# Graph attention and expert block on one core: the second graph's lag in the opening stage goes from two steps to six

## The reference

```python
def gat_layer(x, adj, W, a_self, a_neigh, b):          # twice per batch, 8 heads of 32
    feat = jnp.einsum('nf,hfo->hno', x, W)
    e = attn_self[:, :, None] + attn_neigh[:, None, :]
    e = leaky_relu(e, 0.2) + -1e10 * (1.0 - adj)[None, :, :]
    out = jnp.einsum('hnm,hmo->hno', softmax(e), feat) + b[:, None, :]
    return elu(concat_heads(out))
x = x + graph(ctx_512, layernorm(x))     # adj is the normalised x itself
x = x + block(layernorm(x))              # rmsnorm, q/k/v, rotary, causal attention, out, top-2 of 8 experts
```

## Time and profile before

| | |
|---|---|
| median of 3 runs | 664.06 us (659.31 to 664.84) |
| the profiled execution | 662.46 us, of which the span is 660.7 us |
| opening stage, by the trace | 0 to about 127.6 us of the span |
| TensorE busy over the span | 606.6 us (92%) |
| VectorE busy over the span | 434.6 us (66%) |
| GpSimd busy over the span | 305.9 us (46%) |
| ScalarE busy over the span | 268.6 us (41%) |
| products for the clock (L637) | 131, all between 12.8 and 118 us |

### The profile page before, as it was taken

One profiled execution on the slowest core, in us unless ns is written; L12 is line 12 of the kernel. 1 busy time (PEld: TensorE's weight loads), 2 busy tenths in 40 slices (PEclk: granted clock), 3 DMA queues, 4 the chain that ended last, 5 costly groups with the idle time before them and its releaser, 6 DMA issues.

```text
span 660.7 us, 10362 instructions
## 1 busy us (share of the span) xinstructions
PE 606.6 (92%) x3271; PEld 437.0 (66%) x3271; DVE 434.6 (66%) x1279; ACT 268.6 (41%) x653; POOL 305.9 (46%) x588
## 2 busy tenths in 40 slices
PE   3799899489799999989799999989999998999998
PEld 2278468236586789736597789746768873666886
DVE  4997499389756387689757387655653656664463
ACT  2462563065566333055556333036750204675020
POOL 1493594278853240268854150267730027863000
PEclk9999899799999999998989999999999999999999
DMA  8920000000000000000000000000000000000000
GB/s 276 387 73 2 1 1 4 12 4 2 1 1 0 1 2 1 24 9 1 0 2 1 0 1 1 3 15 1 1 1 0 1 9 8 1 0 1 1 0 17
DMA packets 8729, 14.41 MB, mean 22 GB/s; under 512 B 908, under 2 KB 7372, under 8 KB 8420
## 3 DMA queue, kind: packets, MB, share of 16 engines
q1 hardware_dynamic: 8676, 13.76, 5.9%
HBM read 12.70 MB, written 1.05 MB: 21 GB/s over the span
## 4 chain that ended last, share of the span: by engine, by line
PE 64%; DVE 20%; issue 6%; POOL 4%; ACT 4%; DMA 1%; DVEq 0%; POOLq 0%; SPq 0%; ACTq 0%
PE bank L615 14%; PE bank L513 10%; PE bank L573 6%; PE bank L559 5%; PE bank L592 4%; PE ob L487 4%; PE tb L476 3%; PE bank L637 2%; DVE tt L958 2%; PE bank L588 2%; PE bank L584 2%; DVE ssq L1023 2%; ACT prob L726 2%; DVE m L1020 2%; DVE qT L958 1%
## 5 line engine op out<-in xcount | busy, mean ns | idle before, releaser
L559 PE MATMUL bank<-wqkv_sb,hT 128*128 128x512 f32 x192 | 95.0, 635 | 0.4 <-ACT v_sb L702 0.4
L726 ACT ACTIVATE prob<-bank,sneg,rms 128x128 f32<-128x128 f32 (+1 forms) x128 | 63.9, 508 | 59.6 <-DVE sneg L1052 59.4
L836 POOL TENSOR_TENSOR m<-early,rope_s 128x256 f32<-128x256 f32 x80 | 73.5, 942 | 30.8 <-ACT early L707 30.6
L513 PE MATMUL bank<-m,wgu_sb 128*128 128x128 f32 (+1 forms) x480 | 85.6, 329 | 0.8 <-DVE early L1099 0.8
L794 POOL TENSOR_SCALAR tt<-tt,gmn 128x256 f32<-128x256 f32 x96 | 67.3, 710 | 37.4 <-DVE gmn L958 37.0
L852 POOL TENSOR_SCALAR prob<-prob,srcp 128x128 f32<-128x128 f32 (+1 forms) x128 | 53.1, 432 | 51.4 <-DVE srcp L1123 51.2
L513 PEld LDWEIGHTS bank<-m,wgu_sb 128*128 128x128 f32 x480 | 71.0, 191 | 9.0 <-DVE early L1099 2.2
L573 PE MATMUL bank<-kT,qT 128*128 128x128 f32 (+1 forms) x256 | 61.5, 356 | 1.8 <-ACT prob L726 1.8
L559 PEld LDWEIGHTS bank<-wqkv_sb,hT 128*128 128x128 f32 x192 | 35.9, 199 | 36.9 <-issue 34.0
L615 PE MATMUL bank<-wo_sb,qT 128*128 128x256 f32 x256 | 59.0, 382 | 0.7 <-ACT qT L732 0.7
L707 ACT ACTIVATE early<-bank 128x512 f32<-128x512 f32 x40 | 24.1, 602 | 84.4 <-PE bank L559 84.4
(11 more groups left out here) (200 smaller groups left out, 1217.0 us busy)
## 6 DMA issues: line engine op xcount, KB each, us to landing
wqkv_sb<-wqkv_dram SPq DMA_DIRECT2D x1, 3072.0 KB, 12.0
wgu_sb<-wgu_dram SPq DMA_DIRECT2D x2, 1408.0 KB, 11.5
wo_sb<-wo_dram SPq DMA_DIRECT2D x1, 2048.0 KB, 18.2
wd_sb<-wd_dram SPq DMA_DIRECT2D x1, 1408.0 KB, 15.6
out_dram<-rows SPq DMA_DIRECT2D x8, 128.0 KB, 1.7
xin<-x_dram SPq DMA_DIRECT2D x3, 256.0 KB, 2.7
rows<-gat_rows_dram SPq DMA_DIRECT2D x2, 256.0 KB, 2.8
kT<-x_dram SPq DMA_DIRECT2D x1, 256.0 KB, 4.5
```

The source lines that it names most:

```text
L513: mm = pe.matmul(ps[:, m * N + c0:m * N + c1], wgu_sb[:, m, k, n * P:(n + 1) * P], tokT[:, k, c0:c1], start=(k == 0), stop=(k == KT - 1))
L559: mm = pe.matmul(ps[:, :], hT[:, k, t * P:(t + 1) * P], wqkv_sb[:, k, c * G * HD:(c + 1) * G * HD], start=(k == 0), stop=(k == KT - 1))
L726: ins = act.activation(prob[:, n % 5, i * nk:(i + 1) * nk], ps[:, i * nk:(i + 1) * nk], ACT.Exp, bias=sneg[:, n, i:i + 1], scale=rq(g, t, ...
L836: ins = pool.tensor_tensor(dst[:, :, c, :], src[:, :, 1 - c, :], s_, ALU.mult)
```

## The change

Only constants of the schedule change. Batch 1's graph runs six steps behind batch 0's in the opening stage. The setup of the second layer's term columns is one step earlier (14 and 15). The rotary tables, the mask and the expert rows are made at steps 25, 26 and 27. The unread products are 94 and not 131, with other counts for each step: none at step 43, ten at step 30 and ten at step 47, fourteen at step 8 as before, one where there were two.

```diff
-BEHIND = 2
-TERMS1_AT, ROPE_AT = (15, 16), (39, 40, 41)
-WAKE = {2: 3, 7: 4, 8: 14, 19: 3, 20: 3, 21: 3, 22: 3, 23: 3, 24: 3, 25: 3, 26: 3, 27: 3, 28: 3, 30: 4, 31: 14, 43: 20}
-WAKE.update({s: 2 for s in tuple(range(9, 19)) + tuple(range(32, 43))})
+BEHIND = 6
+TERMS1_AT, ROPE_AT = (14, 15), (25, 26, 27)
+WAKE = {2: 3, 4: 2, 6: 3, 7: 3, 8: 14, 25: 3, 26: 3, 27: 3, 28: 4, 29: 4, 30: 10, 47: 10}
+WAKE.update({s: 1 for s in tuple(range(9, 25)) + tuple(range(31, 47))})
```

## The result

| | before | changed |
|---|---|---|
| median | 664.45 us (4 runs) | 691.44 us (4 runs, 687.41 to 695.46) |
| profiled execution | 662.46 us, span 660.7 | 689.64 us, span 687.8 |
| granted clock over the span | 0.977 | 0.916 |
| `hT` begun (L1007) | 126.6 us | 156.0 us |
| first q/k/v product (L559) | 128.5 us | 160.5 us |

The ratio is 1.0419 (95% interval 1.0346 to 1.0491): the change makes the kernel 4% slower. The forecast was 655 us. The opening stage is 32.0 us longer, and the tails give 4.9 back.

A forecast was written before the change was run, and what follows sets the result against it. VectorE was taken to set the opening stage's pace, GpSimd and TensorE close behind. 7.0 us from the schedule and 1.8 from the clock, 8.8 off 662.46, gave 653.7; 655 was predicted for the median, range 648 to 662.

The forecast's parts named there:

- The start: Opening of layer 0: batch 0's first leaky relu at 16.5 us against 20.51, 4 us earlier.
- The fourteen products at step 8: Unread products before batch 0's fifth unit: 3.0 us at the high clock, 3.5 allowed, VectorE idle some 2.5.
- Steps 9 to 41: Middle of both layers: VectorE sets the pace; batch 0's layer 0 ends at 59.7 us, step 35 at 92.4.
- TensorE's list for these steps: Steps 13 to 18: TensorE's 13.8 us and GpSimd's 12.2 do not bound VectorE's 18.3.
- the last rival: One-graph steps: the clock falls, steps take 3.1 to 4.0 us, 17 us lost, 671; chance 0.09 with other losses.
- I charge nothing for the dropped products.: Whole opening stage: 37 dropped unread products, 8.0 us of TensorE time, counted as covered by VectorE or the turn.
- The turn: Layer 0 to layer 1, steps 19 to 27: batch 1 drains under it, first leaky relu at 74.0 us against 74.58.
- the 7 us promised: End of the opening stage: `hT` ends at 120.5 us against 127.46, 7.0 us earlier from the schedule.
- Rival 1: One-graph steps: GpSimd's 2.03 us a unit sets the pace, 4.4 less gain, 659; 0.31 together with late pair operands or drain.
- The setup's place: Rotary setup, mask and expert rows in the turn: 5.1 us of VectorE, 2.3 us too long for its cover.
- The tails' start: First q/k/v product: 1.98 us at the high clock instead of 3.78, 1.8 us gained from the clock.
- The forecast's own sign of being wrong: Steps 28 to 41: VectorE waiting for unit products or granted clock under 0.9; or the wait before L1001 still near 3.9 us.

The follow-up runs named there:

- lag6_filled_k8: lag6_filled with six instead of fourteen unread products at step 8; median 656.29 us, 0.9886 of the kernel before.
- lag6_filled: lag6_three with twelve instead of three unread products at steps 13 and 27; median 662.04 us, 0.9943 of the kernel before.
- lag2_termsonly: The kernel before with only the term columns made one step earlier (14 and 15); median 670.74 us, ratio 1.0104.
- lag6_three: The changed kernel with three unread products instead of one in steps 9 to 24 and 31 to 46; median 673.89 us, 1.0156 of the kernel before.
- lag2_ropemid: The kernel before with term columns at 14 and 15 and rotary tables, mask and expert rows at 25 to 27; median 670.43 us, ratio 1.0094.
- lag2_ropeonly: The kernel before with only rotary tables, mask and expert rows moved to steps 25 to 27; median 660.94 us, ratio 0.9965.
- lag4_three: lag6_three with a lag of four instead of six; median 664.9 us, 1.0013 of the kernel before.
- lag2_filled: lag2_ropeonly with ten unread products at step 47 and nine at step 29; median 668.06 us, 0.9928 of the kernel before.

## Why the prediction was wrong

*The start* was right: first leaky relu at 16.27 us (16.5 foretold, 20.51 before).

*The fourteen products at step 8* were mis-sized: 4.42 us, not 3.5, and VectorE idle 4.26, not 2.5. By their length a part of them ran at 1.2 GHz, as in the earlier trace rows at step 31. With eight fewer the next unit comes 1.5 us earlier (lag6_filled_k8).

*Steps 9 to 41: the failed step is TensorE's list, priced at the high clock.* "TensorE's list for these steps is 13.8 us with its six unread products ... neither bounds" was computed at 2.4 GHz, and so were the lists of the second layer. At 1.2 GHz a step takes 3.48 us, more than twice VectorE's 1.58. This was the last rival, and its mechanism and its price for a step were right (3.1 to 4.0 us; L487 went to 1.75, near the upper of its two bounds). Wrong were the two things said against it, and its extent. "Idle times in those steps are under 1 us each": at 33 us the clock fell behind pauses of 0.69 and 0.18 us, though at 106 us it did not behind the same two, and at 111 us the pause was 2.41. "The clock stayed at 1.00 from 85 to 98": with two graphs in a step and two unread products, where the changed kernel has one product and in most steps one graph's work. The extent was put at 14 steps of the second layer, 17 us, but both layers ran slow, 34 to 88 and 112 to 160 us; TensorE was busy for 141.00 us and not 102.25, and the stage lost 32. The chance of 0.09 for it was too low by far.

*"I charge nothing for the dropped products."* That was the wrong account: they were charged as TensorE time that VectorE covers, and their worth is the clock. The sparse table at a lag of two costs 2.8%; 64 more products at a lag of six gain about 18 us. In steps 19 to 24 the table went from three to one, not only from two.

*The turn* had the wrong cover. In lag6_filled, at the full clock, layer 1 began 5.2 us later than I had it. I had followed VectorE's order to the microsecond and TensorE's only in sums: batch 0's terms stand behind batch 1's transposes and products in the same step. Of the 7 us promised none was there: `hT` ends at 129.0 and not at 120.5, with two more unread products in each of 32 steps.

*Rival 1* was half right: GpSimd did fall behind, by pair operands of 5.16 us and not of 2.2 to 2.5, and TensorE's pause in front of the second fall of the clock is a wait for it; no row shows that it set VectorE's pace.

*The setup's place.* Hidden in the turn as I said; but the forecast took the term columns' one step for nothing, and at a lag of two that step alone costs 1% (lag2_termsonly).

*The tails' start* was right: 1.98 us for the first q/k/v product at the full clock. The forecast's own sign of being wrong came true, the granted clock under 0.9 in steps 28 to 41 (0.50 from 120 to 150 us). One reading was off without bearing on the sum: the DMA share is not 0.00 all the way after 60 us but 0.07 from 113.2 to 127.6.

The Trainium skill ("TensorE: Matmul & The Clock Gate", The HAM clock gate) states that activity lifts a throttled default. The runs agree so far as unread products raise it (0.68 over the stage with 94 of them, 0.99 in lag6_filled with 176). That TensorE has no pause isn't enough in these runs: it was busy 10.00 of 10 us at 0.50 from 60 to 70 and from 70 to 80.

## What to carry to other kernels

Where unread products hold the clock, their table belongs to one order of the work: after any move look at the granted clock by windows first, and price the stage at both levels before counting which engine bounds it. A row of TensorE with a wait in front and doubled durations behind it is the sign. Filling the two longest pauses, 2.31 and 1.80 us, with 18 products took lag6_three from 673.9 to 662.0 us; 64 products spread evenly had taken 691.4 to 673.9. Moving 1.9 us of another engine's work ahead of the operation that frees a TensorE buffer cost 6.7 us here in one place (lag2_termsonly against the kernel before) and 9.5 in the other (lag2_ropemid against lag2_ropeonly).

## What the runs showed that I had not expected

- The clock stayed at 0.50 while TensorE was busy without a gap: from 38 to 84 us in the changed kernel, with products L487 of 33 columns, transposes and one unread product a step. It rose at 87 to 89 us, during or behind the feature product L458 and four unread products.
- It fell behind pauses of quite different length: 2.41, 2.31, 2.13, 1.80, 1.13, 1.12 us, and 0.48 or 0.69 with 0.18. It held behind others of the same length: 1.13 us in lag6_filled, 0.69 with 0.18 at 106 us in the changed kernel.
- At 1.2 GHz eight products of 33 columns take 1.75 us instead of 0.98, and four transposes 1.06 instead of 0.60 to 0.66.
- Some of these kernels have executions 20 to 40 us apart (lag4_three 663.5 and 703.3; lag2_filled 656.8 and 677.6), while 23 of the kernel before, beside the last two, took 659.9 to 668.9.
